# Turning attention A's probabilities for two tiles with one transfer, out of six slots

## The reference, cut to what matters

```python
logits = jnp.einsum('bhid,bhjd->bhij', q, k) * SCALE
logits = jnp.einsum('bhij,gh->bgij', logits, Wpre)
attn = jax.nn.softmax(logits, axis=-1)
attn = jnp.einsum('bhij,gh->bgij', attn, Wpost)
out = jnp.einsum('bhij,bhjd->bhid', attn, v)
out = out.transpose(0, 2, 1, 3).reshape(b, n, DIM)
return out @ Wout.T + bout
```

## Time and profile before

| | us |
|---|---|
| median of three runs (lowest, highest) | 2229.25 (2225.32, 2232.22) |
| the profiled execution | 2227.8 |
| its span, first to last instruction | 2225.9 |
| busy PE / DVE / ACT / POOL | 2086.6 / 1905.7 / 1736.1 / 876.3 |
| attention A's transfers, first issue to last | 76.6 to 1472.9 |
| share of the span: PE / DVE / ACT | 94% / 86% / 78% |

### The profile page before, as it was taken

How to read it: one execution, slowest core, us unless ns; L and a number is a source line. 1 busy time by engine, 2 the same in 40 slices (tenths; PEclk the granted TensorE clock), 3 DMA queues, 4 the chain that set the end, 5 groups by cost and what they waited for, 6 DMA issues and landing times. The chain is left out here.

```text
span 2225.9 us, 62041 instructions
## 1 busy us (share of the span) xinstructions
PE 2086.6 (94%) x24854; PEld 1428.7 (64%) x24854; DVE 1905.7 (86%) x2598; ACT 1736.1 (78%) x3088; POOL 876.3 (39%) x958
## 2 busy tenths in 40 slices
PE   6799999999999999999999999978779999999977
PEld 4467776777677777767777767665535555655654
DVE  6899998999999999999999999958677788878684
ACT  3789998999899999989999999943357777777623
POOL 4332332332323323223323233244007777777640
PEclk9999999999999999999999999988989999999988
DMA  3799999999999999999999999970041111111001
GB/s 103 117 199 191 195 196 185 197 194 193 193 191 198 195 192 194 196 192 193 196 195 193 192 194 193 196 136 1 19 154 31 31 31 31 31 31 31 20 1 38
DMA packets 1097038, 303.78 MB, mean 136 GB/s; under 512 B 1070256, under 2 KB 1090096, under 8 KB 1096496
## 3 DMA queue, kind: packets, MB, share of 16 engines
q1 hardware_dynamic: 1095888, 299.36, 77.3%
q10 hardware_dynamic: 864, 0.47, 0.1%
HBM read 20.83 MB, written 10.49 MB: 14 GB/s over the span
## 5 line engine op out<-in xcount | busy, mean ns | idle before, releaser
L456 DVE SCALAR_TENSOR_TENSOR a_parts<-a_probs,a_parts 128x1024 f16<-128x1024 f32 x512 | 659.2, 1287 | 81.3 <-ACT a_parts L408 80.3
L367 PE MATMUL a_out_ps<-a_vs,a_pT 128*128 128x128 f16 x4096 | 713.5, 219 | 3.8 <-DMA a_pT<-a_parts 3.8
L369 PE MATMUL a_out_ps<-a_vs,a_pT 128*128 128x128 f16 x4096 | 713.5, 219 | 0.0
L371 PE MATMUL a_out_ps<-a_vs,a_pT 128*128 128x128 f16 x4096 | 713.5, 219 | 0.0
L400 ACT ACTIVATE a_probs<-a_score_ps,a_negmax 128x1024 f32<-128x1024 f32 x512 | 570.8, 1115 | 94.1 <-DVE a_negmax L450 86.4
L450 DVE TENSOR_REDUCE a_negmax<-a_score_ps 128x1 f32<-128x1024 f32 x512 | 621.5, 1214 | 9.9 <-PE a_score_ps L353 7.6
L510 POOL TENSOR_TENSOR a_weighed<-a_own_out,wpost 128x256 f32<-128x256 f32 x256 | 246.7, 964 | 965.3 <-DVE a_parts L456 959.7
L408 ACT ACTIVATE a_parts<-a_probs 128x1024 f16<-128x1024 f32 x512 | 540.0, 1055 | 34.0 <-DMA a_pT<-a_parts 32.5
L367 PEld LDWEIGHTS a_out_ps<-a_vs,a_pT 128*128 128x128 f16 x4096 | 401.3, 98 | 63.5 <-ACT a_own_out L418 3.1
L369 PEld LDWEIGHTS a_out_ps<-a_vs,a_pT 128*128 128x128 f16 x4096 | 401.2, 98 | 59.4
L349 PE MATMUL a_score_ps<-kh,a_qs 128*128 128x512 f16 x1024 | 390.1, 381 | 44.2 <-ACT a_probs L400 35.3
(11 more groups left out here) (233 smaller groups left out, 2234.7 us busy)
## 6 DMA issues: line engine op xcount, KB each, us to landing
a_pT<-a_parts SPq DMA_TRANSPOSE x512, 5.1
b_qs<-q_parts SPq DMA_DIRECT2D x96, 64.0 KB, 1.9
b_ks<-k_parts SPq DMA_DIRECT2D x96, 64.0 KB, 1.9
q_parts<-b_parts SPq DMA_DIRECT2D x32, 128.0 KB, 1.9
k_parts<-b_parts SPq DMA_DIRECT2D x32, 128.0 KB, 1.8
x<-x_dram SPq DMA_DIRECT2D x4, 512.0 KB, 7.5
a_rope<-rope_dram SPq DMA_DIRECT2D x1, 2048.0 KB, 11.7
out_dram<-x SPq DMA_DIRECT2D x4, 512.0 KB, 5.4
```

The costliest lines, as they stand in the source:

```text
L367: pe.matmul(out[:, 0:D], hi, vs[:, b, 0, j, :], start=j == 0, stop=False, skip_group_check=True)
L369: pe.matmul(out[:, 0:D], hi, vs[:, b, 1, j, :], start=False, stop=False, skip_group_check=True)
L371: last = pe.matmul(out[:, 0:D], lo, vs[:, b, 0, j, :], start=False, stop=j == JB - 1, skip_group_check=True)
L456: dve.scalar_tensor_tensor(out=parts[:, T % RING_P, 1, :], in0=probs[:, T % RING_P, :], scalar=PSCALE, in1=parts[:, T % RING_P, 0, :], op0 ...
```

## The change

One transposing DMA now turns tiles T and T + 1, of 128 x 4096 float16, 1 MB. It waits for the low part of tile T + 1 and for the product of tile T - 7. `a_parts` gets six slots of its own ring length RING_H, so `high(T)` waits for the landing of the pair that holds tile T - 6. `a_pT` keeps its eight slots, with a semaphore for each pair, four in place of eight. `a_probs` keeps its four slots.

```diff
-AHEAD_A, RING_T, RING_P = 8, 8, 4
+AHEAD_A, RING_T, RING_P, RING_H = 8, 8, 4, 6
-        parts = st.sb(s, "a_parts", [P, RING_P, 2, SEQ], F16)
+        parts = st.sb(s, "a_parts", [P, RING_H, 2, SEQ], F16)
-        turned = [st.sem(f"a_turned{i}") for i in range(RING_T)]
+        turned = [st.sem(f"a_turned{i}") for i in range(RING_T // 2)]
...
-            eng.wait_ge(turned[T % RING_T], 16 * (T // RING_T + 1))
+            eng.wait_ge(turned[T // 2 % (RING_T // 2)], 16 * (T // RING_T + 1))
...
-            for T in range(TILES_A):
+            for T in range(0, TILES_A, 2):
                 if T >= RING_T:
-                    sp.wait_ge(pv_done, T - RING_T + 1)
-                sp.wait_ge(lo_ready, T + 1)
-                sp.dma_start_transpose(pT[:, T % RING_T].rearrange("p a j q -> p (a j) q"),
-                                       parts[:, T % RING_P].rearrange("p a c -> p (a c)")).then_inc(
-                    turned[T % RING_T], 16)
+                    sp.wait_ge(pv_done, T - RING_T + 2)
+                sp.wait_ge(lo_ready, T + 2)
+                to, own = T % RING_T, T % RING_H
+                sp.dma_start_transpose(pT[:, to:to + 2].rearrange("p r a j q -> p (r a j) q"),
+                                       parts[:, own:own + 2].rearrange("p r a c -> p (r a c)")).then_inc(
+                    turned[T // 2 % (RING_T // 2)], 16)
...
-                if T >= RING_P:
-                    wait_turned(act, T - RING_P)
-                act.activation(parts[:, T % RING_P, 0, :], probs[:, T % RING_P, :], ACT.Copy,
+                if T >= RING_H:
+                    wait_turned(act, T - RING_H)
+                act.activation(parts[:, T % RING_H, 0, :], probs[:, T % RING_P, :], ACT.Copy,
```

More of the change, by code:

```diff
@@ L455, in low @@
                 dve.wait_ge(hi_ready, T + 1)
-                dve.scalar_tensor_tensor(out=parts[:, T % RING_P, 1, :], in0=probs[:, T % RING_P, :], scalar=PSCALE,
-                                         in1=parts[:, T % RING_P, 0, :], op0=ALU.mult,
+                dve.scalar_tensor_tensor(out=parts[:, T % RING_H, 1, :], in0=probs[:, T % RING_P, :], scalar=PSCALE,
+                                         in1=parts[:, T % RING_H, 0, :], op0=ALU.mult,
                                          op1=ALU.subtract).then_inc(lo_ready, 1)
```

## The result

The change takes 2199.68 us (median of 4 runs, 2198.96 to 2200.29) against 2229.83 of the kernel before in the same session: ratio 0.9865, 95% interval 0.9851 to 0.9879. That is 30 us, outside the range of 2203 to 2243 and twice the 14 us of the sum. The profiled execution has a span of 2198.3 us against 2225.9, so 27.6 less.

The account below looks back on a forecast made before the run. The prediction took attention A's full stream of transfers as the bound. Borders at -18 us and start and end at +3.6 gave -14.4 us, so 2215 us, with an 8 in 10 range of 2203 to 2243.

Parts of the forecast that it names:

- The transfers bound the kernel: Attention A: SP's stream of 504 transfers, 2.733 us each, is full and its queue never rests.
- The sign of 5.32 to 5.40 us per pair: If right, SP's row stays unbroken: 256 transfers of 5.32 to 5.40 us each, some 1362 us long.
- The ring's cap of 21.42 us per group: Eight tiles without DMA waits take 21.42 us against a mean of 21.86, so relief gives at most 28 us.
- 256 x 0.07 = 18 us: Borders between transfers in attention A: 256 of 512 go, 0.07 us each, saving 18 us, ends 0 and 35.
- The two transfers' data, the holes and the number of packets stay: Transfer stream: data, holes at instruction fetches and packet count unchanged at 256 x 1 MB, so no time gained there.
- The pair's wait: Pairs land 7.5 us after issue in the median, 9.5 at most; PE has 9.65 us; cost 0 in mid-stage.
- Rival 2: PE waits for pairs ahead of even tiles' products: +10 to +36 us, 2240 to 2265; chance 0.23.
- Start and end, +3.6 us: Attention A's ends: stream starts 2.3 us late, PE has two products after the last landing, +1.3 us.
- Rival 3: SP's queue: borders cost more through a hidden fixed part of the issue; ring bounds, -24 us, 2204; chance 0.07.
- The rule against it: Back-to-back transfers overlap their fixed setup cost, so fewer, larger ones save nothing; the sum would be +3.6 us alone.

Follow-up runs that it names:

- lighter product: 16 of 24 product matmuls per tile, six slots: against the single-transfer kernel with six slots 2198.64 us, against the changed kernel with pairs 2200.97 us.
- halves of the queries: Changed kernel with the next head's queries scaled in two halves, at two steps each of ACT and DVE: 2185.69 us, ratio 0.9821 to before.
- stream alone: Changed kernel with a stretch ahead of attention A where SP alone issues 64 tiles as singles, pairs and fours: 2.490, 4.985 and 9.78 us per transfer.
- two light kernels: Six-slot single-transfer kernel and changed kernel, each with 512 of 1024 columns in high and low parts and 8 of 24 matmuls: 2180.29 and 2152.89 us.
- slots alone: Kernel before with six slots of a_parts in place of four, each tile still turned by its own transfer: 2230.59 us, ratio 1.001.
- halves with single transfers: Kernel before with six slots, single transfers and the next head's queries scaled in two halves: 2236.14 us, ratio 1.0032 to before.
- pairs alone: Changed kernel with four slots of a_parts in place of six: 2503.53 us.
- light ring's singles: Six-slot single-transfer kernel with 512 of 1024 columns in high and low parts and 8 of 24 product matmuls: 2180.29 us.

## Why the prediction was right or wrong

- **The transfers bound the kernel: right**, though one of its grounds didn't carry: a merged row of SP's queue looks unbroken in every kernel here, also in the one that waits for 360 us. SP's own waits show it, and three runs: more slots leave the time where it was, a faster ring gains nothing, and a lighter product with a quarter fewer fetches brings the quiet groups' pace to single transfers. The sign of 5.32 to 5.40 us per pair came true, 5.349, but it tells nothing: the ring's cap is 21.42 / 4 = 5.355.
- **The ring's cap of 21.42 us per group: right**, and reached to the hundredth. Whose it was stood open; PE's 2.635 us per tile was put beside it. The lighter product shows that it is not PE's, and the halves of the queries that the one long step of ACT and DVE makes it.
- **"256 x 0.07 = 18 us" for the borders: this step failed.** The runs showed nothing saved, 2 x 2.490 against 4.985 us. The price of a single transfer's border was read about right, 0.07 against 0.085 with the stream alone. What was taken as given is that the 256 borders that stay keep that price; a pair's costs 0.175.
- **"The two transfers' data, the holes and the number of packets stay", a term put at nothing: this step failed too, and here the gain lies.** The holes stay in number and length; their price doesn't. The stream's loss over its own pace fell from 122 to 78 us, 44 us, of which the ring let 27 through. The rows for it were in part at hand: the earlier trace rows shows the rate at 290 GB/s behind a hole and its end after four slices, and the prediction took that as given in place of asking what ends it; the fetches of 8 KB, a third of all, it didn't count. Averaged over the lone fetches of the two light kernels the burst lasts six slices with single transfers and ten with pairs, so four was a short one. (290 - 218) x 4 x 0.3 us = 86 KB are 0.4 us of the stream, more than the 0.2 us measured around such a fetch, so it is a rough account. In the windows of the earlier trace rows and of the changed kernel a short dip stands at the burst's end, as at a border; in the average of the singles none does. What ends the burst, and why the engines can take 290 there and are otherwise fed 218, stays open.
- **That it came out faster is partly luck.** The stream was the bound, but the two missed steps erred in opposite directions: the forecast took 18 us from the borders, which gave none, and nothing from the holes, which gave 27.
- **The pair's wait: right.** Forecast landings 7.5 and 9.5 us in the median and at most, measured 7.5 and 8.9. The room of 9.65 us held: PE waited once in the middle, 0.3 us. Rival 2 took the backlog of before as given, and it shrank as the stream got faster: from the end of the last low part to the start of its transfer it was 2.1 us in the median and is 0.4.
- **Start and end, +3.6 us: about right at the end, too much at the start.** From the last scaling of queries to PE's last group of products it was 1478.4 - 1427.3 = 51.1 us before and is 1455.05 - 1402.2 = 52.9: +1.8 (forecast 1.3). From the first scaling to PE's first product it was 87.27 - 63.8 = 23.5 and is 89.07 - 65.2 = 23.9: of the 2.3 us that the stream starts later, 0.4 show, since the stream is no longer the bound that would carry them on.
- **What came from elsewhere.** From PE's last product to the end of the program no instruction differs, and yet that stretch took 747.2 us before and takes 742.9 (busy times as in the earlier trace rows, then the granted clock):

```profile
1478.70:2225.90 747.20, 674.73 (x9334) 416.41 (x9334) 551.74 (x1135) 439.45 (x935) 407.32 (x407) 0.94 0.12 36
...
1455.40:2198.30 742.90, 670.10 (x9334) 411.95 (x9334) 551.84 (x1135) 439.58 (x935) 407.34 (x407) 0.95 0.12 36
```

PE's busy time differs by 4.6 us and that of DVE, ACT and POOL doesn't, and the granted clock of the stretch is 0.944 on the mean against 0.953. The other kernels that leave nothing out go either way: 747 to 748 us at 0.943 to 0.944 (slots alone; halves with single transfers), 746 at 0.945 (with the stream alone ahead) and 743 at 0.956 (pairs alone; halves with pairs). Why the clock is granted as it is wasn't tried. So about 4 of the 27.6 us of the spans aren't the transfers'.

- **Rival 3** had the outcome, the full cap and SP waiting for low parts, with a chance of 0.07 and another reason (a hidden fixed part of the issue). The stream alone refutes the reason.
- **The rule against it.** The Trainium skill, page "DMA: Bandwidth & Descriptors", section "Rules for kernel authors", says that the fixed setup cost overlaps with work if transfers are issued early. By that rule fewer borders save nothing, and the stream alone agrees, 2 x 2.490 against 4.985 us. The sum drawn from it, no gain, was wrong all the same, since the gain isn't in the setup.

## What to carry to other kernels

Where a DMA queue hardly ever waits for its data, the stream is the bound even if the waits for its landings are few; ask for the queue's own waits, since a merged row hides its pauses. Then look at what interrupts the stream, not only at its borders, and count every kind of interruption. Widening a transfer pays by what it makes good behind an interruption, and only if the rings around it grow with it (here +2 slots; without them 276 us slower). Once it is relieved, look at once for the next cap: here the quiet groups named it to the hundredth, and a cut of one long step brought another 0.4%, by the ratios of 0.9821 and 0.9865.

## What the runs showed of the hardware

- An instruction fetch of 16 KB stops a stream of transposing DMAs for 1.2 to 1.5 us, one of 8 KB for about 0.6 in the window shown. They cost a full stream of single transfers 0.8 and 0.4 to 0.5 us each: 120 of the one and 56 of the other 122 us of the stage. PE's instruction count is thereby a cost of the DMA engines: the fetches of 16 KB fell from 120 to 88 and 57 as 24 matmuls of the product became 16 and 8, and with 88 the single transfers kept up with the ring at 2.681 us, where they held it at 2.733.
- The fetches don't come at any place of a transfer. Half of the 57 of the light ring's singles start 0.39 to 0.57 us behind the first packet of a transfer, in a period of 2.63, and in the paired kernel of the halves the median is 0.31 in a period of 5.29. The hole thus stands just behind a border in both. Why wasn't tried.
- The stream runs at 218 GB/s within a transfer, with 512 KB, 1 MB and 2 MB alike, and at about 290 behind a hole: for some 1.8 us with 512 KB transfers and 3.0 us with 1 MB ones, averaged over the lone fetches of the light ring (30 and 24).
- Back to back, 512 KB, 1 MB and 2 MB took 2.490, 4.985 and 9.78 us, so a border costs 0.085, 0.175 and 0.16 us.
